# Two mixtures of sixteen experts in tiles of 128 rows, the first of them begun inside the loop of the mixture before it

## What is computed

```python
SUBLAYERS = [FFN0, ATTN, FFN0, FFN1, LINATTN, FFN1]
```

## Time and profile before

| | |
|---|---|
| time, median of 3 runs | 1438.44 us (1433.98 to 1439.25) |
| profiled execution | 1434.23 us, its span 1432.4 us |
| PE busy | 1176.8 us, 82% of the span |
| DVE, ACT, POOL busy | 861.8, 748.4, 696.6 us (60%, 52%, 49%) |
| DMA | 220.10 MB, mean 154 GB/s |
| TensorE's clock granted, mean | 0.93 |

### The profile page before, as it was taken

How to read it: one execution, slowest core, us unless ns; L and a number is a source line. 1 busy time by engine, 2 the same in 40 slices (tenths; PEclk the granted TensorE clock), 3 DMA queues, 4 the chain that set the end, 5 groups by cost and what they waited for, 6 DMA issues and landing times.

```text
span 1432.4 us, 27517 instructions
## 1 busy us (share of the span) xinstructions
PE 1176.8 (82%) x7620; PEld 793.1 (55%) x7620; DVE 861.8 (60%) x2897; ACT 748.4 (52%) x1707; POOL 696.6 (49%) x933
## 2 busy tenths in 40 slices
PE   4399797899999999999689878419999777479994
PEld 3299786222223232222379778417889655357894
DVE  7533666888899999988333565722225696522135
ACT  4255453477767767767445545314445566334441
POOL 3776343213233454524754466563455277635553
PEclk9999998799999999999989999759999988589997
DMA  9687667535435435352357666424568131145586
GB/s 297 169 217 217 181 189 225 161 92 165 138 97 157 136 77 144 98 151 75 89 161 192 174 180 182 135 79 140 169 190 269 48 126 36 48 132 166 176 268 201
DMA packets 176707, 220.10 MB, mean 154 GB/s; under 512 B 25040, under 2 KB 126032, under 8 KB 176560
## 3 DMA queue, kind: packets, MB, share of 16 engines
q1 hardware_dynamic: 144880, 174.80, 43.6%
q0 software_dynamic: 17856, 36.74, 7.5%
q10 hardware_dynamic: 13824, 6.82, 1.6%
HBM read 148.25 MB, written 69.76 MB: 152 GB/s over the span
## 4 chain that ended last, share of the span: by engine, by line
PE 53%; DVE 20%; POOL 8%; issue 6%; DMA 5%; ACT 5%; SPq 2%; DVEq 1%; ACTq 0%; POOLq 0%
PE PS L1483 16%; PE PS L1493 16%; DVE arena L2422 6%; POOL dispatched L807 6%; PE PS L1671 5%; PE PS L1647 5%; PE PS L1461 3%; ACT arena L1195 2%; DVE X L1958 2%; PE PS L1655 2%; PE PS L1633 2%; DVE BST L1948 1%; DMA qk_products<-arena 1%; DVEq L2216 1%; DMA arena<-dispatched 1%
## 5 line engine op out<-in xcount | busy, mean ns | idle before, releaser
L1070 ACT ACTIVATE arena<-PS,arena 128x128 f32<-128x128 f32 (+2 forms) x824 | 295.6, 419 | 368.7 <-PE PS L1483 353.2
L829 POOL DMA_INDIRECT expert_out<-arena x302 | 291.6, 965 | 319.1 <-issue 151.3
L1195 ACT ACTIVATE arena<-PS 128x512 f32<-128x512 f32 x512 | 283.9, 597 | 134.4 <-PE PS L1647 133.5
L1493 PE MATMUL PS<-arena 128*128 128x128 f32 (+1 forms) x2416 | 309.4, 277 | 14.7 <-DVE arena L2227 14.2
L1483 PE MATMUL PS<-arena 128*128 128x128 f32 (+2 forms) x1648 | 314.4, 335 | 4.9 <-ACT arena L1070 3.5
L2422 DVE TENSOR_REDUCE arena<-PS 128x2 f32<-128x1024 f32 x256 | 301.1, 1218 | 26.2 <-PE PS L1657 25.0
L1493 PEld LDWEIGHTS PS<-arena 128*128 128x128 f32 x2416 | 294.7, 193 | 29.0 <-issue 18.8
L2227 DVE TENSOR_TENSOR arena<-PS,arena 128x128 f32<-128x128 f32 (+2 forms) x206 | 73.0, 354 | 312.0 <-PE PS L1493 310.6
L1483 PEld LDWEIGHTS PS<-arena 128*128 128x128 f32 x1648 | 237.8, 197 | 39.3 <-issue 9.1
L807 POOL DMA_INDIRECT dispatched<-arena x192 | 186.0, 969 | 81.7 <-issue 55.7
L1647 PE MATMUL PS<-arena 96*128 96x512 bf16 x512 | 173.0, 389 | 12.7 <-ACT arena L1195 6.7
(11 more groups left out here) (273 smaller groups left out, 1171.7 us busy)
## 6 DMA issues: line engine op xcount, KB each, us to landing
arena<-experts SPq DMA_DIRECT2D x64, 578.0 KB
arena<-experts SPq DMA_DIRECT2D x142, 256.0 KB
qk_products<-arena SPq DMA_DIRECT2D x48, 384.0 KB
arena<-qk_products SPq DMA_DIRECT2D x64, 288.0 KB
YC<-expert_out SPq DMA_DIRECT2D x48, 256.0 KB
dispatched<-FILL SPq DMA_DIRECT2D x32, 322.5 KB, 2.5
arena<-dispatched SPq DMA_DIRECT2D x142, 64.5 KB
arena<-qk_products SPq DMA_DIRECT2D x64, 128.0 KB, 5.1
```

The costliest lines, as they stand in the source:

```text
L829: pool.indirect_dma_start(YK, bass.IndirectOffsetOnAxis(ap=ID[:, s:s + 1], axis=0), YS[:, s, :], None).then_inc(s_yo[r], 16)
L1070: act.activation(bent(f, tau)[:, q, 0:N], bank(q, 0, N), func, bias=bias).then_inc(s_g, 1)
L1195: act.activation(PT[:, G % 2, j, k, :], bank(4 + k % 2), ACT.Exp, scale=float(1.0 / np.sqrt(HD))).then_inc(s_exp, 1)
L1493: mm = pe.matmul(bank(6, P * s, P * s + P), bent(f, tau)[:, q, P * s:P * s + P], downs(f, tau, q), start=(q == 0), stop=(q == FC - 1))
```

## The change

FFN1 becomes a mixture with 79 tiles of 128 rows (8192 / 128 + 15), by the same code as FFN0:

```diff
-MOE = [dict(E=E0, S=S0, tiles=TOKENS * 2 // (S0 * P) + E0 - 1), dict(E=E1, S=MAIN, tiles=2 * E1)]
+MOE = [dict(E=E0, S=S0, tiles=TOKENS * 2 // (S0 * P) + E0 - 1), dict(E=E1, S=S0, tiles=TOKENS * 2 // (S0 * P) + E1 - 1)]
-FRONTS = 4
+FRONTS, LAST_FRONTS = 4, 6
+KNOWN1, SOON1 = 5, 25
+REST = 12
```

```diff
+                    if carries(L) and 0 <= tau - soon < 3 * E1 and (tau - soon) % 3 == 0:
+                        wide_stays((tau - soon) // 3)
```

The fourth sublayer's tile 0 stands in step NEXT of the third's loop, twelve steps behind its last tile (70 is the last, so tile 0 is in step 83), and its first 11 tiles run in that loop, between what is left of the routing:

```diff
+        NEXT = MOE[0]["tiles"] + REST
+
+        def tile_at(L, c):
+
+            f = ffn_of(L)
+            if c < moe_of(f)["tiles"]:
+                return f, c
+            if carries(L) and c >= NEXT:
+                return f + 1, c - NEXT
+            return None
...
+            if carries(L):
+                if b >= NG - 2:
+                    return MOE[0]["tiles"] + 3 + 5 * (b - NG + 2)
+                return max(tiles_to(b) + 8 + b, early_tiles(L) + E0 + 6 + 4 * b)
...
         def last_step(L):
-            return place_of(L, NG - 1)
+            return place_of(L, NG - 1) + 4
```

So b6 and b7 start in steps 74 and 79 and have their places in 84 and 89. The table's parts stand on DVE in the step of the place of b4 plus one and two (first table: steps 70 and 71) and of b7 plus one to three (whole table: steps 90 to 92). The gates (`kept_gates`) move behind four tiles:

```diff
+                        if c == place_of(L, KNOWN1 - 1) + 2:
+                            first_rows(f + 1)
+                    tile_out(c - 1)
...
+                        if c == place_of(L, NG - 1):
+                            score_gap(f + 1)
+                        if c == place_of(L, KNOWN1 - 1) + 1:
+                            first_sums(f + 1, bank(5, 0, KNOWN1 * E1))
+                        if c == place_of(L, NG - 1) + 1:
+                            main_counts(f + 1, bank(5, 0, NG * E1))
...
+                    if handed(L) and c == begin(L) + 4 or L == len(SUBLAYERS) - 1 and c == 8:
+                        kept_gates()
```

POOL sends the first 40 (b0 to b4) in the third sublayer, one behind each scatter, and the other 24 between the scatters of the fourth:

```diff
+                    if handed(L):
+                        while sent < 2 * NT and place_of(L - 1, sent // (2 * GT)) <= NEXT + tau:
+                            send_next(L, sent)
+                            sent += 1
                     scatter(tau)
...
-                    if carries(L) and tau < tiles - 8 and place_of(L, sent // (2 * GT)) <= tau:
-                        send_next(sent)
+                    if carries(L) and sent < early and place_of(L, sent // (2 * GT)) < tau:
+                        send_next(L + 1, sent)
```

In the linear attention DVE has `first_table` after the fifth place. The sixth sublayer's tiles 0 to 24 wait for the first 40 sends alone; its whole table stands in its steps 2 to 4. Fronts: in the fourth sublayer at steps 50, 55, 60 and 65 of 79, in the sixth six instead of four, so that only b6 and b7 are gathered after the tiles:

```diff
         def front_of(b):
 
-            return late_to(b) + 6
+            return max(wide_to(b) + 10, 50 + 5 * b)
...
-                    if i == 0:
-                        moments(FRONTS - 1)
-                        inverse_deviation(FRONTS - 1)
...
+                    if i == KNOWN1:
+                        first_table(f, bank(4, 256, 256 + KNOWN1 * E1))
```

More of the change, by code:

```diff
@@ L1121, in first_middle @@
                     act.activation(QP[:, 1, w, :], QR[:, w, :], ACT.Copy).then_inc(s_mid0, 1)
-                for c in range(begin(L), last_step(L) + 1 if carries(L) else tiles):
-                    if c < tiles:
-                        gelus(c)
+                for c in range(begin(L) + handed(L), last_step(L) + 1 if carries(L) else tiles):
+                    gelus(c)
                     if prepares(L):
```

765 lines of the change are left out of this document (391 added, 374 removed).

## The result

The changed kernel takes 1444.96 us (median of 14 runs, 1440.44 to 1452.81), the kernel before 1438.88 in the same runs (14, 1433.62 to 1441.31). The ratio is 1.005, with a 95% interval of 1.0031 to 1.0069: half a per cent slower, which is 6 us by the medians and 7 by the ratio, where 1440 (+2 by the sum) was forecast. The profiled execution took 1443.4 us, its span is 1441.6 us, 9.2 more than that of before.

A forecast was written before the change was run, and what follows sets the result against it. PE bounds the full stretches (fourth and sixth sublayers), chains of waits the empty ones before them and at the end. Terms sum to +2.1 on 1434.2, 1436.3, plus 4.2 for the median: 1440 us, range 1421 to 1458.

The forecast's parts named there:

- C: Fourth sublayer: narrow tiles plus routing, table, exponential, gates and four fronts (gathers, statistics, root) take 186.0 us; with B +3.5.
- G: The end: two batches instead of four combined after the last tile, one round less, −7.1 us.
- A tile's price: Narrow tiles take 2.03 us each; 79 take 160.4 us against 149.1 for the wide ones, +11.3 a mixture.
- A: Memsets beside eight early tiles: halves over twice the steps should fit into the slack, −3.6 us.
- B: Start of the fourth sublayer: eight sends behind the last scatter, first hidden layer at 937, 29 us earlier.
- D: Linear attention: a first table added on DVE, part of a front removed, 4.5 us of which half counts, +2.5.
- F: Sixth sublayer: narrow tiles, table, exponential, gates and six pairs of gathers take 170.8 us against 151.3, +19.5.
- H: Third sublayer: the 16 resident loads, 5.3 MB, should be hidden by rows and weights loaded ahead, +2 us, bounds 0 and 19.
- Rival 2: Third sublayer: resident loads on SP's queue delay weights and stall PE, marked by DMA share above 0.95; 1457 us, chance 0.10.
- Rival 1: Added DVE work beside tiles is hidden in 1.0 us of cover a step; some 1424 us, chance 0.26.
- Rival 3: Hand-over into the fourth sublayer, steps 83 to 93: DVE waits and clock falling with each stall; 1456 us, chance 0.15.
- Rival 4: Fourth sublayer's early start does not come, gaining 15 us instead of 29; 1454 us, chance 0.05.

The follow-up runs named there:

- experiment 9: The changed kernel with the sixth sublayer's first tile waiting for all 64 sends again: 1459.77 us, ratio 1.0152 to the kernel before.
- experiment 1: The kernel before with only its memsets halved (16 instead of 8): 1433.12 us for 1437.93, ratio 0.9966.
- experiment 4: The changed kernel with Newton roots beside tiles cut into halves or thirds, one part a step, ACT's rows three steps later in the fourth sublayer: 1430.22 us, ratio 0.9949.
- experiment 7: The changed kernel with four fronts in the last mixture in place of six, so four batches are combined behind the last tile: 1444.84 us, ratio 1.0056.
- experiment 8: The changed kernel with the sixteen resident parts loaded at sixteen tiles in a row in place of every third: 1448.28 us, ratio 1.0075.
- 4 to 6: The changed kernel with roots in parts (1430.22 us), then also the first table behind tile 70's output (1429.27), then also gates and whole table in pieces (1417.07).
- 3: The changed kernel with the third mixture's first tile six steps behind the second's last in place of twelve: 1451.33 us, ratio 1.0105.
- the kernel of 6: The changed kernel with first table behind tile 70's output and roots, gates and whole table in pieces: 1417.07 us, ratio 0.9864 to the kernel before.
- 11: The kernel of 6 with six steps in place of twelve between the mixtures: 1422.46 us, ratio 0.9891 to the kernel before.

## Why the prediction came out as it did

The forecast was on the right side, and the mechanisms of the starts, the tile price and the bursts on DVE held. By the medians the kernel is 5 us slower than forecast, above all by the sizes of two terms, the fronts in C and the end in G. Some of that closeness is luck. Span for span the sum was short by 7.1 us (+9.2 for +2.1). The median came nearer because 4.2 us had been added for the gap between the profiled execution and the median of before, and for the changed kernel that gap is 1.6. Inside the sum, fronts that cost 4.9 more than their term stand beside first steps that cost 2.9 less and resident parts that cost nothing for +2.

**What bounds.** Right: gains in empty stretches, losses in full ones. Both starts came within 1.4 us of what was worked out, and experiment 9 gives the second one's price from the other side (15 us of time for a forecast of 14.7, though the start itself moved by 17).

**A tile's price.** Right. In the sixth sublayer, away from anything added (durations, first and last start of 41 outputs; DVE's idle time ahead of them):

```profile
L2275 DVE TENSOR_TENSOR arena<-PS,arena x41: 291/292/293, 1281.3 to 1362.7; 128x128 f32<-128x128 f32 x41
...
  PE PS L1511: 41.9, 41
```

81.4 us for 40 steps, 2.035 each against 2.03, and 1.02 us of slack on DVE in each.

**A.** Sized right at the third sublayer's start (−3.5). The first sublayer itself ends 6.2 us earlier (233.2 for 239.4); 2.7 of it are lost again by the time attention is through (2.6 in experiment 1), and no run here shows where.

**B.** The table before tile 70's output: 5.5 us forecast, 5.6 measured (8.87 between the last two outputs for 3.29). The start was 1.4 us less of a gain than forecast, and two sizes behind it were off against each other. "Then 4.9 to the first turn as before" was 6.3 (923.51 to 929.82), and 8.9 to tile 1's turn, which `hidden` of tile 0 also stands behind: SP reads each tile's row from the table before it issues the load (landed at 925.94, issued at 927.07 and, for tile 1, at 928.82), where before eight loads went out one behind the other from 960.88, 0.02 us after the landing. From that turn to `hidden` it was 2.3, not 4.

**C.** The failed size. The fronts' term, "Four fronts of 2.5: 10.0", was 14.9: 55.6 us for 20 steps (experiment 4's first row) against 40.7. Front by front it looks different. Here are the outputs beside the fronts of b1 and of b2, five steps each:

```profile
L2275 DVE TENSOR_TENSOR arena<-PS,arena x6: 291/292/293, 1060.7 to 1077.9; 128x128 f32<-128x128 f32 x6
```

```profile
L2275 DVE TENSOR_TENSOR arena<-PS,arena x6: 291/292/293, 1077.9 to 1090.1; 128x128 f32<-128x128 f32 x6
```

Against 10.2 us for five free steps, b2's front costs 2.1, and so does b3's: the term's 2.5 was right, even a little high. But b0's costs 3.8 and b1's 7.0. Only for these two does ACT scale the rows, two steps behind the gather, right behind a step's gelus, and it waits for the root; the term had nothing for this. At b1:

```profile
1072.02 1.65 ACT L1050 ACTIVATE XS<-X,LN 128x128 f32<-128x128 f32 x4 [3.75 <-DVE LN L2006]
1073.58 1.11 ACT L1091 ACTIVATE arena<-PS,arena 128x128 f32<-128x128 f32 x4
```

```profile
1069.59 0.16 DVE L1998 TENSOR_SCALAR LN<-LN 128x4 f32<-128x4 f32 x1
...
1071.83 0.16 DVE L2006 SCALAR_TENSOR_TENSOR LN<-LN 128x4 f32<-128x4 f32 x1
...
1077.86 0.29 DVE L2275 TENSOR_TENSOR arena<-PS,arena 128x128 f32<-128x128 f32 x1 [4.24 <-PE PS L1511]
```

The root ends at 1071.99 and ACT, idle for 3.75 us, starts its 1.65 us of rows then; the next four gelus start at 1073.58, and PE has nothing to multiply. The output at 1077.86 comes 5.15 us after the one before it. At b0 the same wait makes a step of 3.55 us (after b2, the step there takes 1.92), so it costs 1.6 us each time. The other 1.6 at b1 are the clock: after PE had been busy for 1.07 of the 3.7 us before, it is granted at its lower level, 1.2 GHz, and the 16 products of the step take 3.65 us for 2.05 at b0.

```profile
1074.17:1077.59 3.42, 3.42 (x17) 3.42 (x18) 0.00 (x0) 1.99 (x7) 0.54 (x1) 0.50 0.25 55
```

The last 1.7 us stand in b1's first two steps, in which PE also has the linear sublayer's first turn and products (0.61 us from 1060.53 and 1.73 from 1063.03 in the chain); that is the opening of the linear sublayer, which the kernel before has among its wide tiles too, and not a front's price. Experiment 4 cut these roots and moved ACT's rows away from them at once, so it does not say which of the two gave the 6.6 us at b0 and b1.

The rest of C was a little less than forecast: the first twelve steps cost 4.8 us over their tiles (forecast, 5.8 and 1.9), and the gates 2.75 (forecast 2.7), seen as the step of 4.98 us up to 975.53, in which output 13 waits behind the last gate, and the short one of 1.83 behind it:

```profile
974.29 0.42 DVE L2322 SCALAR_TENSOR_TENSOR GATE<-arena 128x32 f32<-128x32 f32 x2
975.39 0.20 DVE L2272 TENSOR_TENSOR arena<-arena,CST 128x1 uint32<-128x1 f32 x1 [0.68 <-DVE GATE L2322]
975.53 0.29 DVE L2275 TENSOR_TENSOR arena<-PS,arena 128x128 f32<-128x128 f32 x1
...
976.30 0.16 DVE L2272 TENSOR_TENSOR arena<-arena,CST 128x1 uint32<-128x1 f32 x1 [0.28 <-issue]
```

The exponential cost what the row said: in the sixth sublayer it starts at 1263.01 and the next gelu at 1264.55 (chain above), 1.5 us with one table load of 1.28. With the load ahead of it, from 1261.71, it is 2.84 us for both switches. The drain of 1.4 us at each switch that the Trainium skill has, and that the prediction weighed ("ScalarE: Activation LUTs", What ACT_TABLE_LOAD costs), is not in the trace.

**D.** +3.4 for +2.5, within its bounds (half of 4.5 is 2.25; the 2.5 was rounded up). As the linear sublayer moves by up to 5 us from one profile to the next, neither figure is tested.

**F.** +21.1 for +19.5 (its terms add up to 170.7, not 170.8); the six fronts' gathers cost 3.2 us in 30 steps, not 1.8: a gather of 1.13 us is just over the slack, and a step with one takes 2.35 us.

**G.** The second failed size. The prediction gave the two extra fronts 7.1 us; experiment 7 shows that they give 0.5 at the end and nothing in the time. It left out that the first pair of batches can be combined while the last scatter lands. In the kernel before, the chain has two loads of rows behind the last scatter, ahead of the batches at 1421.41 and 1428.54; with four narrow fronts it has one (experiment 7), and the first gather starts at the last output. So with narrow tiles those rows are complete and loaded before the last tile. The likely reason is the order of the tiles, in which the blocks of late batches come last; no run isolates it.

**H.** +2 forecast, a guess between its bounds, nothing measured: 70 outputs take 183.7 us with the resident parts and 183.9 without, and even with all of them in sixteen tiles in a row (8) no wait for weights showed on PE. The total hides one difference: the step up to output 12 takes 6.89 us for 5.23, and TensorE's clock is granted at 0.50 for 3.4 us of it, from 749.90; why it falls there in the changed kernel and not before is open. Rival 2 is out, and so is its mark of 0.95: in experiment 8 the share was 0.94 to 1.00 with PE full. The Trainium skill ("DMA: Bandwidth & Descriptors", Queues, rings and completion order) has descriptors of one ring consumed in order; no run here shows the weights delayed by a resident part: six tiles of them are loaded ahead, and PE waited for none.

**The rivals.** Rival 1 (the added work is hidden) did not hold for the change as it was written, and came largely true when the bursts were cut (4 to 6: 1417 us, for the 1424 of the rival). Rival 3, the rough hand-over, did not hold: the first twelve steps were cheaper than forecast. The clock was at 0.50 until 941.05, about the first output, but did not fall back with each stall: it stayed at 1.00 until 1074.17, also through the gates' step of 4.98 us. Rival 4 did not hold: the start came 27.7 us earlier.

**The twelve steps.** That twelve steps are better than six is shown by 3 (8 us) for the changed kernel; for the kernel of 6 the profiles of 11 point the same way (6.8 us in outputs 0 to 48), and the intervals overlap. The prediction had taken twelve as given and did not price it.

## What to carry to other kernels

Work on an engine that is not the bottleneck is free only in pieces no longer than the idle time of one step: read that idle time from the rows (here 1.0 us of a 2.03 us step), and cut chains of small dependent instructions to it. The same 12-instruction root beside b2 made a step of 3.33 us in one piece, and steps of 1.94 and 2.19 us and a part of 3.02 in three. Put the pieces where no other burst stands in the step: the third part met the next gather and was not free. And ask who waits for the moved piece on a third engine: beside b1, ACT waiting for DVE in front of its gelus, and the clock that fell with PE's stall, cost 3.2 us, more than the 1.3 of the root itself. When a chain of sends is made shorter, look for the next one behind it before adding gains up: two changes of 6 and 14.5 us gave 15.

## What the runs showed that had not been expected

Ahead of a tile's output DVE loads a table entry into a register. Where that load has to wait until the DVE instruction before it is done (`TENSOR_LOAD arena [waits dve_step]` in the order of the change, and behind every gather), the trace shows 0.68 us idle (the row at 912.12 above, `[0.68 <-DVE arena L2176]`; also at 975.39 behind the gates). Where it has nothing to wait for and runs beside a tile's copy, it shows 0.28 to 0.36. This adds to every burst that stands directly ahead of a tile's output, and is part of why a gather of 1.13 us overruns a slack of 1.0. No run moved the load, so what that would give is open.

TensorE's clock is a part of many of these differences. It falls in one execution and not in another of the same code: through the gates' step, in which PE idles for 2.48 us, it stays at 1.00 in the changed kernel, and in experiment 7, whose fourth sublayer is the same code, it is at 0.50 for 3.4 us from 973.74. A difference of a few us between two profiles is worth reading against the granted clock of the stretch before it is put down to an edit.
